# A routed expert stage: one half's remainders carried into the other half's blocks, and top two from the logits

## The reference

```python
h = residual + mamba_block(rmsnorm(x_n))        # d_inner 256, 16 states, scan over 512 tokens
hs = rmsnorm(h).reshape(-1, 128)                # 2048 tokens
router_logits = hs @ router_w                   # 8 experts
rw = softmax(router_logits); top_w, sel = top_k(rw, 2)
for e in range(8):
    w_e = where(sel == e, top_w, 0).sum(-1)
    ye = (silu(hs @ Wg[e]) * (hs @ Wu[e])) @ Wd[e]     # 128 -> 512 -> 128
    out = out + w_e[:, None] * ye
x = x + (h + out)
x = x + ffn(layernorm(x))                       # gated, 128 -> 384 -> 128
x = x + latent_attention(layernorm(x))          # 16 heads, causal
```

## Time and profile before

| what | value |
|---|---|
| median of 3 runs | 688.85 us (685.72 to 689.6) |
| profiled execution, its own time | 688.8 us |
| its span in the profile | 687.0 us |
| PE / DVE / ACT / POOL busy, share of the span | 83% / 69% / 58% / 47% |
| first scatter of the first half | at 217.0 us |
| expert blocks | 278 to 440 us |
| first score maximum of attention | at 440.4 us |

### The profile page before, as it was taken

One profiled execution on the slowest core, in us unless ns is written; L12 is line 12 of the kernel. 1 busy time (PEld: TensorE's weight loads), 2 busy tenths in 40 slices (PEclk: granted clock), 3 DMA queues, 4 the chain that ended last, 5 costly groups with the idle time before them and its releaser, 6 DMA issues.

```text
span 687.0 us, 11539 instructions
## 1 busy us (share of the span) xinstructions
PE 570.7 (83%) x3652; PEld 379.7 (55%) x3671; DVE 475.6 (69%) x1266; ACT 400.9 (58%) x666; POOL 324.6 (47%) x285
## 2 busy tenths in 40 slices
PE   2967899678677887889989999757799989988887
PEld 1423343224254564879989899625545545544466
DVE  4759997998789987536335653587777878886052
ACT  2677657756755776556756656314356556656731
POOL 5259988895996994225785324412011112112010
PEclk9979999899897999999999999957999999999999
DMA  5845455443755453201152003232003003000001
GB/s 142 305 167 159 150 186 154 143 129 109 241 183 160 142 135 100 68 16 36 54 133 86 20 17 105 68 100 58 9 25 87 10 20 92 4 3 3 1 16 47
DMA packets 49085, 63.32 MB, mean 92 GB/s; under 512 B 7570, under 2 KB 29090, under 8 KB 48770
## 3 DMA queue, kind: packets, MB, share of 16 engines
q1 hardware_dynamic: 43682, 56.65, 27.5%
q0 software_dynamic: 2496, 5.15, 2.1%
q10 hardware_dynamic: 2848, 0.78, 0.5%
HBM read 44.84 MB, written 9.52 MB: 79 GB/s over the span
## 4 chain that ended last, share of the span: by engine, by line
PE 36%; DVE 9%; issue 7%; ACT 4%; POOL 3%; DMA 1%; ACTq 1%; POOLq 0%; another core or an unknown queue 0%; DVEq 0%
PE ps L1792 33%; DVE arena L1712 3%; ACT arena L1296 2%; POOL moe_rows L899 1%; DVE stats L1383 1%; PE ps L2153 1%; DVE x L1647 1%; POOL moe_out L907 1%; DVE nb L1396 1%; ACT r L1296 1%; DMA moe_out<-arena,xT 1%; PE ps L2160 1%; ACT arena L1316 1%; ACT arena L1304 1%; ACTq L1286 1%
## 5 line engine op out<-in xcount | busy, mean ns | idle before, releaser
L1792 PE MATMUL ps<-arena 128*128 128x128 f32 (+11 forms) x2147 | 329.2, 329 | 42.9 <-DVE arena L1712 17.9
L1792 PEld LDWEIGHTS ps<-arena 128*128 128x128 f32 (+2 forms) x2166 | 209.0, 157 | 130.2 <-issue 59.3
L1574 DVE TENSOR_TENSOR_SCAN arena<-ps,arena 128x512 f32<-128x512 f32 x128 | 149.8, 1210 | 21.4 <-ACT ps L1225 15.2
L926 POOL TENSOR_TENSOR arena<-arena 128x1024 f32<-128x1024 f32 x64 | 127.9, 2016 | 25.5 <-DVE arena L1561 19.8
L1792 PE MATMUL ps<-arena,ident 128*128 128x512 f32 x216 | 109.5, 644 | 30.9 <-DVE arena L1586 30.8
L1712 DVE CUSTOM_DVE_ANT_0 arena<-ps,cmask 128x128 f32<-128x128 f32 (+3 forms) x256 | 111.5, 488 | 26.4 <-PE ps L1792 25.2
L1225 ACT ACTIVATE ps<-arena 128x512 f32<-128x512 f32 x128 | 87.4, 689 | 47.2 <-DVE arena L1574 45.5
L1792 PEld LDWEIGHTS ps<-arena,ident 128*128 128x128 f32 x216 | 42.4, 207 | 85.9 <-issue 44.2
L1296 ACT ACTIVATE arena<-ps 128x1024 f32<-128x1024 f32 (+3 forms) x86 | 57.0, 709 | 38.0 <-PE ps L1792 37.6
L907 POOL DMA_INDIRECT moe_out<-arena,xT x46 | 44.9, 976 | 66.5 <-DVE arena L1736 57.1
L1766 DVE TENSOR_TENSOR arena<-arena,ps 128x512 f32<-128x512 f32 x46 | 31.6, 688 | 57.1 <-PE ps L1792 43.6
(11 more groups left out here) (220 smaller groups left out, 700.3 us busy)
## 6 DMA issues: line engine op xcount, KB each, us to landing
arena<-bc_rows SPq DMA_DIRECT2D x118, 256.0 KB, 3.7
arena<-arena SPq DMA_DIRECT2D x64, 64.0 KB
arena<-arena SPq DMA_DIRECT2D x28, 128.0 KB, 2.4
moe_rows<-arena SPq DMA_DIRECT2D x2, 1495.0 KB, 11.8
arena<-moe_rows SPq DMA_DIRECT2D x8, 325.0 KB, 4.3
arena<-in_L_attn_a_Wg SPq DMA_DIRECT2D x8, 256.0 KB, 4.2
arena<-in_L_attn_a_Wu SPq DMA_DIRECT2D x8, 256.0 KB, 4.8
arena<-moe_out SPq DMA_DIRECT2D x4, 512.0 KB, 4.5
```

The lines of the kernel that those rows point to most:

```text
L926: G.tensor_tensor(dBx[:, g % RING, :, :], dx[:, :, cs], bs[:, g % BS, :].unsqueeze(1).to_broadcast([P, CT, L]), ALU.mult).then_inc(s_dbx, 1)
L1574: V.tensor_tensor_scan(hst[:, g % STATES, e, :], bank(6 + e), dBx[:, g % RING, e, :], 0.0, ALU.mult, ALU.add).then_inc(s_scan, 1)
L1792: return T.matmul(o, l, rr, start=start, stop=stop)
```

## The change

The second half no longer rounds each expert up apart from the first. The first half's rows fill exactly 16 blocks: all the full ones of each expert, and of the remainders those that are largest, until 16 are reached. Rows that don't fit get slots in the first 8 blocks of the second half, one for each expert (whose expert is therefore known when the program is built); the second half has 25 blocks. The first 24 blocks are stored in order by SP, and the first half's outputs are then gathered by slot, 16 indirect transfers on POOL. Only the second half's 25 blocks are scattered by token, and in its first 8 the rows of the first half are sent to a row that nobody reads.

The two largest are taken from the logits in PSUM; the exponentials, and the weights from them, follow later off that path. Events move: in the scan `top` at state 43, `fill_blocks` 45, `first_slots` 47, `top_weights` 50; in the expert stage as below. The second half's scatters stand in one run ahead of all puts.

```diff
-        NBLK = TH * 2 + NE - 1
-        CH = (0, 3, 8, 13, 18, NBLK)
+        FIRST = 2 * TH
+        LEFT = P * max((FIRST - f) * (f - TH) // NE for f in range(TH, FIRST + 1))
+        SECOND = (FIRST * P + LEFT + NE * (P - 1)) // P
+        NBLK = FIRST + SECOND
+        CH = ((0, 3, 8, 12, FIRST), (0, 3, 10, 23, SECOND))
...
-                    "top_a": first_1 + 11, "top_b": first_1 + 13, "rank": first_1 + 14, "slots": first_1 + 15}
+                    "top": first_1 + 11, "rank": first_1 + 12, "fill": first_1 + 13, "slots": first_1 + 15,
+                    "weights": first_1 + 18}
...
-        steps, later, use = [], [], []
+        steps, later, use = [("f_down", 1), ("f_add", 1)], [], []
...
+        in_moe = {0: [("h2norm",), ("h2turn", 0)], 1: [("h2turn", 1)], 2: [("route",), ("top",)], 3: [("rank",), ("slots",)],
+                  6: [("exps",)], 8: [("weights",)], 10: [("add_r", 0)], 11: [("add_r", 1)], 12: [("add_r", 2)],
+                  13: [("add_r", 3)], 18: [("targets",)],
+                  28: [("combine", 0), ("f_norm", 0, 0)], 29: [("f_normalise", 0, 0)], 30: [("f_turn", 0, 0), ("f_low", 0, 0)],
+                  33: [("combine", 1), ("f_norm", 0, 1)], 34: [("f_down", 0), ("f_normalise", 0, 1)], 35: [("f_add", 0), ("norm", 0)],
+                  36: [("normalise", 0), ("f_turn", 0, 1), ("f_low", 0, 1)], 37: [("turn", 0)],
+                  38: [("qk", 0, 0)], 39: [("qk_rest", 0, 0), ("qk", 0, 1)], 40: [("qk_rest", 0, 1), ("vals", 0)]}
+        tile_after = {31: (0, 0), 32: (0, 1), 33: (0, 2), 37: (1, 0), 38: (1, 1), 39: (1, 2)}
+        GATHER_AT = (25, 29)
...
+            for i in range(NBLK):                      # SyncE
+                if i == LOAD_1:                        # 12
+                    load_blocks(1)
+                if i < FIRST + NE:
+                    store_block(i)
...
+            for t in range(TH):                        # POOL, ahead of all puts
+                for k in range(2):
+                    scatter(1, t, k)
...
+            for i in range(FIRST + 1, NBLK):
+                put_block(i - 1)
+                if i == GATHER_AT[0]:
+                    for j in range(TB):
+                        for k in range(2):
+                            gather(0, j, k)
+                if GATHER_AT[1] <= i < GATHER_AT[1] + TB:
+                    for k in range(2):
+                        gather(1, i - GATHER_AT[1], k)
+                attend(parts, in_moe.get(i, []))
...
+            def gather(b, j, k):
+                G.indirect_dma_start(got[b][:, j, k, :], None, first_out,
+                                     bass.IndirectOffsetOnAxis(ap=slotu[:, 0, k, TB * b + j:TB * b + j + 1], axis=0)
+                                     ).then_inc(s_ga[b], 16)
...
+            def top(h):                                # DVE; logits lie in PSUM
+                V.tensor_tensor(mk[:, 0:TH, :], req[0], req[1], ALU.add).then_inc(s_mk, 1)
+                V.tensor_tensor(wtok[:, sl, NE:NE + 2], rmax[:, sl, 0:2], rmax[:, sl, 0:1].to_broadcast([P, TH, 2]),
+                                ALU.subtract).then_inc(s_rs2, 1)
...
+            def fill_blocks(ranks):                    # key, above and nblk: key lies in SBUF, above and nblk in PSUM
+                V.scalar_tensor_tensor(key_base[:, :], tot, float(NE), iota8[:, :], ALU.mult, ALU.add)
+                ch.link(V.tensor_tensor(scmp[:, 0:NE, :], tot.unsqueeze(2).to_broadcast([P, NE, NE]),
+                                        iota_full[:, :].unsqueeze(1).to_broadcast([P, NE, NE]), ALU.is_ge))
+                ch.link(V.tensor_reduce(full[:, :], scmp[:, 0:NE, :], AX, ALU.add))
+                V.tensor_reduce(nfull[:, :], full[:, :], AX, ALU.add)
+                ch.link(V.scalar_tensor_tensor(key, full[:, :], -float(NE * P), key_base[:, :], ALU.mult, ALU.add))
+                ch.link(V.tensor_tensor(scmp[:, 0:NE, :], key.unsqueeze(1).to_broadcast([P, NE, NE]),
+                                        key.unsqueeze(2).to_broadcast([P, NE, NE]), ALU.is_gt))
+                ch.link(V.tensor_reduce(above, scmp[:, 0:NE, :], AX, ALU.add))
+                ch.link(V.tensor_scalar(took[:, :], above, nfull[:, 0:1], float(FIRST), ALU.add, ALU.is_lt))
+                ch.link(V.tensor_tensor(nblk[:, :], full[:, :], took[:, :], ALU.add))
+                ch.link(V.tensor_tensor_scan(incl[:, :], ones8[:, :], nblk[:, :], 0.0, ALU.mult, ALU.add))
```

More of the change, by code:

```diff
@@ L198, in build @@
         mk = carve([TH + 1, NE], BF16)
-        iota_b = carve([NBLK])
-        iota_p = carve([NE])
+        iota_b = carve([SECOND - NE])
+        iota_full = carve([NE])
+        iota_carry = carve([NE])
+        iota_rest = carve([NE])
+        full = carve([NE])
+        nfull = carve([1])
+        key_base = carve([NE])
+        took = carve([NE])
+        limit = carve([NE])
+        jump = carve([NE])
+        carried = carve([NE])
+        carry_at = carve([NE])
+        carry_room = carve([NE])
         ridx = carve([NT, 8], U32)
@@ L208, in build @@
         nblk = ps[:, 4, 96:96 + NE]
+        key = carve([NE])
+        above = ps[:, 4, 112:112 + NE]
+        past = ps[:, 4, 192:192 + TH * NE].rearrange("p (t e) -> p t e", t=TH)
         incl = carve([NE])
@@ L365, in build @@
         s_sc = [sem(f"rows_scattered{h}") for h in range(2)]
[L366 removed]
+        s_xg = [[sem(f"block_rows_loaded{h}_{q}") for q in range(len(CH[h]) - 1)] for h in range(2)]
         s_xt = sem("block_transposed")
@@ L376, in build @@
         s_yst = [sem(f"block_output_stored{k}") for k in range(YR)]
+        s_ypt = [sem(f"block_output_put{k}") for k in range(YR)]
+        s_nb2 = sem("second_token_numbers")
         s_ga = [sem(f"outputs_gathered{b}") for b in range(NB)]
@@ L440, in o_bank, with half_of, rows_of, stores_before @@
             return 6 if b == NB - 1 and qt % 2 else 7
+        def half_of(i):
+            return (0, i) if i < FIRST else (1, i - FIRST)
+        def rows_of(h, a, b):
+            if h == 0:
+                return xg0[:, a:b, :]
+            return xg1[:, a:b, :] if b <= CH[1][-2] else xg2[:, a - CH[1][-2]:b - CH[1][-2], :]
+        def stores_before(i):
+            return len([n for n in range(min(i, FIRST + NE)) if n % YR == i % YR])
+        def puts_before(i):
+            return len([n for n in range(FIRST, i) if n % YR == i % YR])
+        def expert_of(eng, i):
+            h, k = half_of(i)
+            if h and k < NE:
+                return slice(k, k + 1)
+            if k == (NE if h else 0):
+                eng.wait_ge(s_eb, h + 1)
+            n = k - NE if h else k
+            return bass.ds(eng.value_load(ebt[0:1, h, n:n + 1], min_val=0, max_val=NE - 1), 1)
         def tiles_of(h):
@@ L946, in _ @@
                 scatter(0, j // 2, j % 2)
-            powers(2 * TB, 2 * TB)
+            for b in range(HB, NB):
+                powers(TB * b, TB)
+            pool.wait_ge(s_sc[0], 16 * 2 * TH)
+            ch.link(G.iota(numbers[:, :, D], pattern=[[2 * P, TH]], base=0, channel_multiplier=2,
+                           allow_small_or_imprecise_dtypes=True))
+            G.iota(unused[:, :], pattern=[[1, SECOND]], base=2 * NTOK, channel_multiplier=SECOND,
+                   allow_small_or_imprecise_dtypes=True).then_inc(s_nb2, 1)
             def clear_keys(b):
@@ L1191, in copy_ahead @@
                     moe_input(c)
-                elif what == "logits":
-                    logits(0)
                 elif what == "exps":
@@ L1617, in _ @@
                     count["var"] += 1
-                if g == ROUTE_AT["top_a"]:
-                    top_a(0)
+                if g == ROUTE_AT["top"]:
+                    top(0)
+                if g == ROUTE_AT["fill"]:
+                    fill_blocks(rank_bank(0))
                 if g == ROUTE_AT["slots"]:
-                    find_slots(0, rank_bank(0))
+                    first_slots(rank_bank(0))
+                if g == ROUTE_AT["weights"]:
+                    top_weights(0)
             weigh(NST - 1)
@@ L1728, in _ @@
             parts = dict(norm=norm, normalise=normalise_block, f_norm=f_norm, f_normalise=f_normalise, f_low=f_low, qk_rest=rest_part,
-                         maxima=maxima, o_add=finish, h2norm=lambda: h2_norm(1, asked_h2), top_a=lambda: top_a(1),
-                         top_b=lambda: top_b(1), slots=lambda: find_slots(1, rank_bank(1)), add_r=add_r, combine=combine,
+                         maxima=maxima, o_add=finish, h2norm=lambda: h2_norm(1, asked_h2), top=lambda: top(1),
+                         slots=lambda: second_slots(rank_bank(1)), weights=lambda: top_weights(1), add_r=add_r, combine=combine,
                          targets=targets)
@@ L2024, in block_turn @@
             def block_turn(i):
-                h, k = divmod(i, NBLK)
-                for q in range(len(CH) - 1):
-                    if k == CH[q]:
-                        pe.wait_ge(s_xg[h][q], 16)
+                h, k = half_of(i)
+                if k in CH[h]:
```

(1 more changed line is left out.)

299 lines of the change are left out of this document (161 added, 138 removed).

## The result

The changed kernel takes 691.86 us, median of 20 runs (687.9 to 695.91), the kernel before 688.58 in the 20 runs beside them: ratio 1.005, 95% interval 1.0027 to 1.0072. It is slower by half a per cent, where the forecast was 687 against 688.85. The profiled execution took 695.4 us (span 693.6), 3.5 above its median.

What follows compares the result with a forecast made beforehand. Limit changes by stage: POOL in the scan's second half, PE in steady expert blocks. Terms -13.95 +3.0 -3.6 -3.4 +7.7 +1.8 +5.6 +0.9 gave -2 us, so about 687 against 688.85, range 674 to 693.

Steps and rivals of the forecast that it cites:

- first routing: First half's routing in the scan: VectorE operations with two SBUF inputs wait for POOL, slots come +3.0 us later.
- blocks without scatters between them: Expert stage: VectorE no longer waits for block outputs queued on POOL behind scatters, -3.4 us.
- five blocks fewer: Expert stage bound by PE: five blocks at 2.79 us each go, -13.95 us.
- `top_weights(0)` in the scan: Second half of the scan: its work and port wait fall into VectorE's slack, nothing; 2.7 us if there were none.
- The clock: PE's lower clock after the new stands at the combines: 0 to 3.6 us, taken as +0.9.
- second routing: Second half's routing in the early expert blocks: PE loses 4.75 us in place of 8.4, -3.6 us.
- Gathers: At both combines VectorE waits 4.1 and 3.8 us, PE stands 10.8 in place of 3.1 us: +7.7 us.
- Query and key rows: End of the expert stage: PE waits in shared blocks, +1.8 us; SP's later row transfers delay attention, +5.6 us.
- Rival C: At the combines, gathers cost POOL more than 1.6 us each; slower, 692 us at 1.6; chance 0.12.
- D: Blocks go but attention starts no earlier, rows being placed later or the clock lower for long: 689 us; chance 0.08.
- A: At the combines, gathers don't hold VectorE, being cheaper on POOL or faster to land: -10.5, 678 us; chance 0.2.
- B: In the first routing, the port wait doesn't bite: -3.75, 683 us; chance 0.15.

Runs made afterwards that it cites:

- e2_weights: The changed kernel with the reciprocal of `top_weights` kept in PSUM, so its product has one SBUF input; ratio 1.0137 to the kernel before.
- c4_after: The changed kernel itself, run again as control of the last set, on a chip without stops; 691.37 us, ratio 1.0051 to the kernel before.
- e12_no_chain: Changed kernel plus routing and weight operands in PSUM, four key transfers on ScalarE, POOL paced by VectorE's block outputs; combines and tiles not moved; 686.17 us, ratio 0.9984.
- e1_fill: The changed kernel with operands of the first half's routing put in PSUM; ratio 1.0103 to the kernel before.
- c_after: The changed kernel itself, run again as control on a chip with stops; ratio 1.0152 to the kernel before.
- e8_pace: The changed kernel with POOL waiting for VectorE's block outputs between pairs of scatters and of gathers; 700.82 us, ratio 1.0022 to the kernel before.
- e11_gathers: Changed kernel plus PSUM operands, ScalarE key transfers, POOL pacing, moved combines and tiles, second batch's gathers at blocks 31 to 34, ones at 27; 678.68 us, ratio 0.9853.

## Why the forecast was wrong

Right in size were the first routing (+3.0 said, +2.0; 0.6 of the difference is that the scans ended earlier, 195.58 against 196.22), the blocks without scatters between them (-3.4 said, -3.6), and five blocks fewer at 2.79 us each.

*`top_weights(0)` in the scan: "nothing".* This step failed. The price was known ("if VectorE had none, 2.7") and the slack was read from a sum, 38.85 us busy of 43.00. But a sum over 43 us says nothing of one moment. At 229.9 the chain of state sums went through VectorE, and 2.04 us there held PE. Measured by `e2_weights`: 1.0 to 3.3 us, mean 1.8, the clock's share in it included.

*The clock: +0.9.* This failed most. The forecast gave half of the earlier trace rows's 1.8 us for the stretch after the second stand, and nothing for the first, whose cost would only shorten the second wait. That wait did come out shorter (3.06 for 3.8), but the stretches took 2.0 + 3.0 = 5.0 us (4.7 in `c4_after`). In the profile of the result another, at 288.6, takes 1.7 us of the 3.6 that the second routing was to give. In `c4_after` it is missing, and the stage gives 2.6. Between 230 and 440 us the granted clock stood at 0.50 for 27 us in the profile of the result and 17 in `c4_after`, before the change for 3.4. The earlier trace rows had shown the price: three short waits cost 1.8 us.

*Gathers: PE stands 10.8 us.* Right: 10.3. The 1.27 us taken from the scatter is 1.25. VectorE's waits are 5.56 and 3.06 against 4.1 and 3.8; the first is longer because the store of block 23 was queued on SyncE behind the transfers of ones and zeros (POOL waited 1.47 us for it), a queue that the forecast did not look at.

*Query and key rows.* The forecast put the first maximum 24.8 us after block 38 starts; it is 24.5 and 24.0. Of the two terms' 7.4 us the trace shows 9.3, as what is left of 21.45 (7.5 + 13.95) when 12.2 more than before is lost at the combines (10.3 + 5.0 in place of the 3.1 that the forecast counted before).

*Second routing: -3.6.* It gave -1.1 and -2.6. The sum took 8.4 us off, where its own terms give 32.6 - 24.4 = 8.2. By idle time and lower clock PE loses 7.0 us between blocks 0 and 12 before the change, and 5.7 after it (4.1 in `c4_after`).

The errors add up: +3.3 (scan), +3.6 (combines: 4.1 more by the clock, 0.5 less by the stands), +2.5 (second routing), +1.9 (end), less 1.0, 0.2 and 1.5 by the first, fourth and sixth rows, make the 8.6 us between -2 and +6.6. Against the medians the error is 5 us. The second profile is close to the median of its runs (690.93 against 691.37); there the errors are +1.1 (scan), +4.9 (block 25 to the first maximum, 3.8 of it clock) and +1.0 (second routing), less 1.1, 0.2 and 1.5, about 4.2 us. So the clock term, put at 0.9 and measured at 4.7 to 5.0, turned the forecast gain into a loss, and `top_weights(0)`, put at nothing, is the second failure. Rival C, the only one that was slower, named 692 but for a dearer gather, and that was false. D (689: attention starts no earlier, or the clock is lower for long) had a chance of 0.08 and is the nearest by mechanism: the first maximum came at 448.5 and 444.0 in place of 440.4. A (gathers don't hold) is ruled out by VectorE's waits of 5.56 and 3.06 us and again by `e12_no_chain`, B (the port wait doesn't bite) by `e1_fill`.

## What to carry to other kernels

Slack is a property of a moment: before an operation is put into an "idle" engine's queue, look in the timeline at what stands right behind it, and give it at most one SBUF input while POOL computes. Price a stand of PE with the slow stretch behind it, here 2 to 3 us on top of 4 to 6. When work moves to indirect transfers, write down POOL's queue as a whole, small arithmetic on which a chain hangs included, and let POOL's pace hang on another engine's progress: that cost 0.5 to 0.8 us in blocks 12 to 25 where it was not needed, and gave some 10 us where it was (700.8 against the 710.6 and 711.3 of other sets' controls).

## What the runs showed of the hardware

- During rows of indirect transfers by POOL with pauses of only 0.30 us, VectorE, ScalarE and TensorE stopped for up to 13.8 us on four of the five chips of these sets, and on the fifth never, with the same kernel and the same 0.96 us for each transfer on POOL. Two stages of the kernel before are 15.4 us longer there, two of the changed one 20.6. What came late were semaphores of the engines' own finished work, by up to 16.2 us (`c_after`). With pauses in POOL's row (`e8_pace`) no stop with a late signal was over 3 us.
- An indirect gather costs POOL what an indirect scatter costs: 0.94 to 0.99 us and 0.30 between two.
- VectorE operations of 128x8 to 128x64 elements take 0.14 to 0.23 us, and 1.2 to 2.0 when both inputs are in SBUF and POOL has a product running; each gets in where one of POOL's operations ends.
- Best version: `e11_gathers`, 1.5% under the kernel before and 1.8% under the changed one (678.68 against 688.58 and 691.37). It keeps the change's 41 blocks and its routing.
